# Graph network on one core: first score row spread by a product, constants taken behind the first exponentials, and identity products around seven stage boundaries

## The reference

```python
# network 0: x1 = relu(x @ W_ah + b_ah); three attention layers (4 heads of 192) on the same x1
h = (x1 @ W).reshape(N, H, C)
e = leaky_relu((h * a_src).sum(-1)[src] + (h * a_dst).sum(-1)[dst], 0.2)
p = exp(e - segment_max(e, dst)[dst])
out = segment_sum((p / (segment_sum(p, dst)[dst] + 1e-16))[:, :, None] * h[src], dst) + b
x = layernorm(x + relu(concat(relu(out_0), relu(out_1), relu(out_2)) @ W_out + b_out))
# network 1: one such layer with 4 heads of 512, elu, one with a single head of 768
x = layernorm(x + gat(elu(gat(x, heads=4, d=512)), heads=1, d=768))
```

## Time and profile before

| | us |
|---|---|
| median of 3 runs (1964.57 to 1966.22) | 1965.33 |
| the profiled execution | 1964.74 |
| its span | 1963.0 |
| TensorE busy in it | 1817.6 (93%) |
| VectorE busy | 1445.3 (74%) |
| ScalarE busy | 1034.1 (53%) |
| mean granted TensorE clock | 0.968 of 2.4 GHz |

### The profile page before, as it was taken

The page is one execution under the profiler, slowest core; times in us unless marked ns, Lnnn a source line. Parts: engine busy times, 40 slices in busy tenths (PEclk is TensorE's granted clock), DMA queues, the critical chain, the costliest instruction groups (busy, mean ns, idle before and its releaser), DMA issues. The chain is left out here.

```text
span 1963.0 us, 30340 instructions
## 1 busy us (share of the span) xinstructions
PE 1817.6 (93%) x11217; PEld 1754.5 (89%) x11217; DVE 1445.3 (74%) x2468; ACT 1034.1 (53%) x1631; POOL 135.3 (7%) x132
## 2 busy tenths in 40 slices
PE   7999899995999999997999899969999996999898
PEld 5777689995999999996999799969999996999798
DVE  7787659998989988984555559447888885346756
ACT  3666522215798898875211322257788874232633
POOL 5011022110000000000011011100000000000000
PEclk8999999997999999997999999989999998999899
DMA  4122154445284344537654566472342406545302
GB/s 123 52 62 67 35 154 138 116 118 133 62 210 100 100 110 101 132 72 197 182 172 147 143 188 192 141 190 66 118 140 68 133 27 183 166 122 129 101 9 79
DMA packets 181465, 234.72 MB, mean 120 GB/s; under 512 B 76102, under 2 KB 154288, under 8 KB 181083
## 3 DMA queue, kind: packets, MB, share of 16 engines
q1 hardware_dynamic: 173215, 205.31, 38.1%
q0 software_dynamic: 7216, 24.91, 4.4%
q10 hardware_dynamic: 902, 2.72, 0.5%
HBM read 167.89 MB, written 65.00 MB: 119 GB/s over the span
## 5 line engine op out<-in xcount | busy, mean ns | idle before, releaser
L1639 PE MATMUL p_o<-p_hi,h_parts 125*128 125x416 f32 (+1 forms) x960 | 282.7, 355 | 22.0 <-DVE p_lo L1573 15.5
L1089 PE MATMUL p_o<-first_room,p 125*125 125x193 f32 x1200 | 202.7, 330 | 13.2 <-DVE p L1045 10.4
L1089 PEld LDWEIGHTS p_o<-first_room,p 125*125 125x125 f32 x1200 | 197.9, 190 | 14.8 <-issue 14.3
L1639 PEld LDWEIGHTS p_o<-p_hi,h_parts 125*128 125x128 f32 x960 | 181.7, 189 | 28.2 <-issue 15.7
L1089 PE MATMUL p_o<-h_in,p 125*125 125x193 f32 x1200 | 198.1, 327 | 0.8 <-ACT res L976 0.8
L1089 PEld LDWEIGHTS p_o<-h_in,p 125*125 125x125 f32 x1200 | 196.0, 188 | 2.3 <-ACT res L976 1.2
L756 DVE CUSTOM_DVE_ANT_0 max_junk<-src_row,G 125x1250 bf16<-125x1250 f32 x120 | 186.2, 1623 | 9.9 <-DMA src_row<-score_rows 9.3
L1040 DVE TENSOR_TENSOR e<-e 125x1250 f32<-125x1250 f32 x120 | 174.3, 1452 | 20.0 <-ACT e L1002 19.9
L855 PE MATMUL p_h<-pw_hi,x1T 128*125 128x384 f32 x720 | 186.4, 340 | 0.0
L1045 DVE SCALAR_TENSOR_TENSOR p<-e,CT 125x1250 f32<-125x1250 f32 x120 | 175.3, 1461 | 4.1
L1375 PE MATMUL p_h<-pw_hi,x2T 128*125 128x256 f32 (+1 forms) x960 | 173.1, 282 | 0.0
(11 more groups left out here) (255 smaller groups left out, 3863.3 us busy)
## 6 DMA issues: line engine op xcount, KB each, us to landing
f_raw<-turned SPq DMA_DIRECT2D x40, 500.0 KB, 8.8
h_rows<-h_out SPq DMA_DIRECT2D x32, 560.0 KB
h_parts<-h_rows SPq DMA_DIRECT2D x40, 448.0 KB
turned<-tail_room SPq DMA_DIRECT2D x18, 625.0 KB, 7.3
G<-turned SPq DMA_DIRECT2D x20, 562.5 KB
h_rows<-h_out SPq DMA_DIRECT2D x24, 424.4 KB
first_room<-in_w_gat POOLq DMA_DIRECT2D x36, 192.0 KB, 2.7
first_room<-in_w_gat SPq DMA_DIRECT2D x6, 1152.0 KB
```

The lines of the kernel that those rows point to most:

```text
L1089: last = nc.tensor.matmul(p_o[:, b, n * 256:n * 256 + C0 + 1], p[:, g % RING, d * T:(d + 1) * T], h_in[hh][:, s, 0:C0 + 1], start=(s == 0 ...
L1639: last = nc.tensor.matmul(p_o[:, bank(n, c), 0:w], h[:, s, kind, cols].bitcast(F32R), pp[:, g % RING, 0:w], start=(s == 0 and j == 0), sto ...
```

## The change

Four kinds of edits.

- **First row.** In `project`, row 0 of the scores is spread by three f32 products of `rows` with column 0 of the identity as a broadcast stationary, and a copy by ScalarE into `src_row`, in place of its way over DRAM. Row 1 alone is still loaded by ScalarE's queue, now behind that copy. The split of `wa0` moves from the start of `project` on VectorE to the end of `counts_and_x1`.
- **Constants behind the first exponentials.** `aggregate_layer0` no longer waits for its bias before the first exponential; `aggregate_layer1` makes `ones` behind its first pair and `b_minus` behind its fourth. `project_layer1` has one extra exponential of a column at its 21st tile (`exp_of_one`), so that the activation table is there when `aggregate_layer1` begins. `aggregate_last` takes its first pair of exponentials before it rounds h, and the first `p_lo` before the next step of VectorE.
- **Identity products.** `keep_busy` writes ident x ident into a PSUM bank that nothing reads then: 8 at the end of stage 1; 12 at the start and 6 at the end of stage 3; 7 and 28 at those of stage 4; 9 and 40 at those of stage 6; 11 at the start of stage 7; 16 at the start of stage 8.
- **Constants of stage 1.** `ident_b` and `zeros_b` become slices of `band` (two memsets and a select less on GpSimd), and two small tiles lie in `G`'s room.

```diff
+def keep_busy(nc, ident, out, n):
+    for _ in range(n):
+        nc.tensor.matmul(out, ident[:, 0:out.shape[0]], ident[:], start=True, stop=True)
...
 # counts_and_x1, vector, at the end
+            dve.wait_ge(weighed.summed, weighed.chunks * 2 * weighed.heads)
+            v.tensor_copy(wa_hi[:], wa_flat).then_inc(wa_rounded, 1)
+            dve.wait_ge(wa_rounded, 1)
+            v.tensor_tensor(wa_lo[:], wa_flat, wa_hi[:].bitcast(F32), ALU.subtract)
...
 # project, scalar
             act.dma_start(score_rows[0:R, :], rows[:]).then_inc(rows_stored, 16)
+            act.wait_ge(row_spread, 1)
+            for b, (at, n) in enumerate(CH):
+                last = a.activation(src_row[:, 0, at:at + n], p_r[0:T, b, 0:n], ACT.Copy)
+            last.then_inc(row_in[0], 32)
             act.wait_ge(rows_stored, 16)
-            for h in range(2):
-                dma_in_two(act, src_row[:, h, :], score_rows[h:h + 1, :].broadcast_to([T, N]), row_in[h])
+            dma_in_two(act, src_row[:, 1, :], score_rows[1:2, :].broadcast_to([T, N]), row_in[1])
...
 # project, tensor
-            pe.wait_ge(wa_split, 1)
...
             last.then_inc(rows_turned, 1)
+            for b, (at, n) in enumerate(CH):
+                last = nc.tensor.matmul(p_r[0:T, b, 0:n], ident[0:R, 0:1].broadcast_to([R, T]), rows[:, at:at + n],
+                                        start=True, stop=True)
+            last.then_inc(row_spread, 1)
...
 # aggregate_layer0, scalar: the wait moves into keep(), in front of the first copy that needs the bias
-            act.wait_ge(bias_in, 16)
...
+                if i == 0 and c == 0:
+                    act.wait_ge(bias_in, 16)
...
 # project_layer1, scalar
+                if n == 2 * NT:
+                    a.activation(table_ahead[:], ident[0:T, 0:1], ACT.Exp)
...
 # aggregate_layer1, tensor, at the end (the other calls of keep_busy stand first or last in their lists)
+            pe.wait_ge(left, (ENDS - 1) * CW)
+            keep_busy(nc, core.ident, p_o[:, bank(ENDS - 2, CW - 1), 0:128], 40)
...
 # aggregate_last, vector
-                if g and s != 1:
+                if g == 0:
+                    rest_of_h(0)
+                    rest_of_p(0)
+                elif s != 1:
                     rest_of_p(g - 1)
                 add(g)
-                if s == 1:
+                if g == NT + 1:
                     rest_of_p(g - 1)
```

More of the change, by code:

```diff
@@ L217, in _ @@
                                pattern=[[1, NT]], channel_multiplier=-1).then_inc(later_ready, 1)
-            for m in (band, ident_b, zeros_b):
-                pool.memset(m[:], 0.0).then_inc(consts, 1)
-            pool.wait_ge(consts, 6)
-            pool.affine_select(out=ident_b[:], in_=ident_b[:], compare_op=ALU.not_equal, fill=1.0, base=0,
-                               pattern=[[-1, T]], channel_multiplier=1).then_inc(consts, 1)
+            pool.memset(band[:], 0.0).then_inc(consts, 1)
+            pool.wait_ge(consts, 4)
             pool.affine_select(out=band[:], in_=band[:], compare_op=ALU.not_equal, fill=1.0, base=N - T,
@@ L251, in _ @@
             step(v.scalar_tensor_tensor(meets[:, 0, :], least, tile_lo[:, 1:2], meets[:, 0, :], ALU.is_lt, ALU.mult))
-            step(v.scalar_tensor_tensor(meets[:, 1, :], run_no_i[:], float(-ER), meets[:, 0, :], ALU.add, ALU.mult))
-            step(v.scalar_tensor_tensor(meets[:, 2, :], run_no_i[:], 1.0, meets[:, 0, :], ALU.add, ALU.mult))
+            step(v.scalar_tensor_tensor(meets[:, 1, :], run_no_i, float(-ER), meets[:, 0, :], ALU.add, ALU.mult))
+            step(v.scalar_tensor_tensor(meets[:, 2, :], run_no_i, 1.0, meets[:, 0, :], ALU.add, ALU.mult))
             step(v.tensor_reduce(out=range_f[:, 2:3], in_=meets[:, 1, :], axis=AX.X, op=ALU.min))
@@ L787, in _ @@
             for b, (at, n) in enumerate(CH):
-                last = a.activation(rows[:, at:at + n], p_r[:, b, 0:n], ACT.Copy)
+                last = a.activation(rows[:, at:at + n], p_r[0:R, b, 0:n], ACT.Copy)
             last.then_inc(rows_kept, 1)
@@ L1491, in _ @@
             a = nc.scalar
-            act.wait_ge(ones_set, 1)
-            a.activation(ones[:], ones_f[:], ACT.Copy).then_inc(ones_set, 1)
-            act.wait_ge(bias_in, 16)
-            a.activation(b_minus[:], b_col[:], ACT.Copy, scale=-1.0).then_inc(bias_in, 16)
-            act.wait_ge(bias_in, 32)
             def round_p(g):
@@ L1533, in _ @@
                 last.then_inc(exp_ready, 1)
+                if g == 0:
+                    act.wait_ge(ones_set, 1)
+                    a.activation(ones[:], ones_f[:], ACT.Copy).then_inc(ones_set, 1)
                 if g:
                     round_p(g - 1)
+                if g == 3:
+                    act.wait_ge(bias_in, 16)
+                    a.activation(b_minus[:], b_col[:], ACT.Copy, scale=-1.0).then_inc(bias_in, 16)
+                    act.wait_ge(bias_in, 32)
                 if n and 4 <= s < 8:
@@ L1615, in sum_weights @@
             def sum_weights(g, n, s, w):
+                if g == 0:
+                    pe.wait_ge(ones_set, 2)
                 if s == 0:
@@ L2225, in _ @@
                 last.then_inc(exp_ready, 1)
-                if g:
+                if g == 0:
+                    round_h(0)
+                    round_h(1)
+                    round_p(0)
+                if g > 1:
                     round_p(g - 1)
@@ L2310, in _ @@
                 part, s = divmod(g, NT)
-                if part == 0:
+                if part == 0 and s:
                     rest_of_h(s)
@@ L2424, in gnn_two_layers @@
                 core.wa0 = sb1("wa0", [128, KD, 2, CONVS * H0], F32)
+                core.wa0_parts = [sb1(f"wa0_{name}", [128, KD, 2 * CONVS * H0], F32R) for name in ("hi", "lo")]
                 core.x1T = [sb1(f"x1T{i}", [128, KD, N], F32R) for i in range(2)]
                 counts_and_x1(nc, core, src, dst, x, w_ah, b_ah, w_gat0, a_gat0)
-                project(nc, core, core.x1T, w_gat0, core.wa0, h0_rows, score_rows, PAIR, cols[0:2], *cols[2:4])
+                project(nc, core, core.x1T, w_gat0, core.wa0_parts, h0_rows, score_rows, PAIR, cols[0:2], *cols[2:4])
             tail = ctx.enter_context(ExitStack())
```

53 lines of the change are left out of this document (31 added, 22 removed).

## The result

The changed kernel took 1957.13 us in the median of 7 runs (1954.44 to 1960.61), against 1966.88 for the kernel before in the same session (7 runs, 1964.57 to 1972.98): a ratio of 0.9948, 95% interval 0.9933 to 0.9962, 9.75 us or 0.5%. The profiled execution took 1956.66 us (span 1955.0), 8.1 less than that of before. The prediction had 17.85 us off that execution and 1947.5 us in all; the time came down as forecast, but by about half as much.

The account below looks back on a forecast made before the run. TensorE bounds the kernel, busy 1817.6 of 1963.0 us. Terms 5.1+1.8+2.3-0.2+3.15+1.7+4.0=17.85 off 1964.74 give 1946.9, plus 0.6 for the median 1947.5 us; range 1944 to 1951, 66 in 100.

Parts of the forecast that it names:

- Boundary 1 to 2 and stage 2, 5.1 us: Stage 2: first maximum 7.9 us earlier, TensorE's last tile 0.3 later, stage 3 begins 5.1 us earlier (2.5 to 6.5).
- Stage 3, 1.8 and 2.3 us: Start of stage 3: 1.8 us from not waiting for the bias, 2.3 us from the clock held by 12 identity products.
- The bias term: Start of stage 3: the first exponential no longer waits for `b_col`, 1.8 us gained.
- The clock term: Start of stage 3: 12 identity products spare TensorE's first products the 1.2 GHz clock, 2.3 us gained.
- Boundary 3 to 4 and stage 4, -0.2 and 0: Six products cost 0.2 us at the boundary; stage 4's faster start is worth nothing, as TensorE waits for `f_lo`.
- Stage 5, 0: Boundary 4 to 5: 28 products end beside SP's last stores; stage 5's first product hangs on VectorE: 0 (-0.3 to +0.3).
- Stage 6, 3.15 and 1.7 us: Start of stage 6: TensorE starts 3.15 us earlier with constants behind the exponentials; the held clock gives 1.7 us more.
- drain: Stage 6's table load: a skill's rule adds some 1380 ns, making the term 1.4 us larger; the prediction's trace disagreed.
- Stage 7, 0: Start of stage 7: 2.75 us at the low clock is worth nothing, as TensorE waits for `f_lo` behind a DMA.
- Stage 8, 4.0 us: Start of stage 8: 3.2 us earlier start, 1.75 us of clock, a 0.9 us wait; net 4.0 us (3.2 to 4.2).
- The identity products don't hold the clock: Rival, 14 in 100: in stages 2, 3, 6 and 8 only earlier starts count, 10.4 us, 1954.9 us.

Follow-up runs that it names:

- e8: The changed kernel without the six identity products ending stage 3 and the seven beginning stage 4: ratio 0.9959.
- e13: The kernel before with only the score-vector split moved to the end of stage 1 and the new stage 1 constants, first row over DRAM: 0.9986.
- e5: The kernel before with only the constants behind the first exponentials, the extra exponential in stage 5 and the new order of stage 8: 0.9957.
- e3: The changed kernel with all nine groups of identity products taken out: 0.9940.
- e10: The changed kernel with the first row over DRAM, first-head divisors ahead of the sums of weights, and no identity products: 0.9916.
- e18: The changed kernel run again unchanged, its third profile: 0.9957.
- e2: The changed kernel with VectorE making the first head's divisors ahead of two sums of weights: 0.9929.
- e4: The kernel before with only the nine groups of identity products put in: 0.9989.
- e7: The changed kernel with the first row sent over DRAM again: 0.9935, 1953.15 us.
- e15: The changed kernel with the first row over DRAM, first-head divisors first, and only the identity products 9, 40 and 11 of stages 6 and 7: 0.9942.

## Why the prediction was wrong, by its own steps

**Boundary 1 to 2 and stage 2, 5.1 us.** The steps held: first maximum at 260.82 (261.5 forecast), the new products at 2.35 us (3.8), VectorE's end 449.1 (450), SP's stores behind the last tile as what ends the stage. The term measured 3.5, 0.7 and 4.1 us in three profiles. What was too small was the delay of TensorE's tiles, 0.3 us forecast and 1.1, 4.1 and 0.9 measured from the stage's start; the range of the term, 2.5 to 6.5, missed one of three. In that one the new products ran at the low clock and took 4.50 us, in the others 2.35 and 2.34. The eight products behind stage 1 did not keep the clock either: it was at 0.50 for the first 3 us of stage 2 in two of the three (241.0 to 244.4 in the first).

**Stage 3, 1.8 and 2.3 us.** This is the step that failed: "VectorE needs 2.87 us for a step and TensorE 3.27, so the lead is not eaten." The rates are right and the conclusion is not, because the lead is eaten at the change of head, where TensorE waits for divisors and copies. From its first product to the second head it took 36.21 us (to 0.01) in all thirteen profiles that had VectorE's old order, whatever the clock was. I had read the waits there as for "VectorE or ScalarE work that follows its own products (bank copies)"; the 0.81 us of before followed VectorE's list. The bias term measured 1.42. The clock term measured not +2.3 but -2.7 to -3.1 against the first profile of before (-1.7 to -2.1 against the second), since the longer wait let the clock fall once more. In the profiled execution that is 5.0 of the 9.8 us that were missing (17.85 less 8.1).

**Boundary 3 to 4 and stage 4, -0.2 and 0.** -0.17 at the boundary. Stage 4 took 2.1 to 2.7 us more. The waits came for `fw_lo`, ahead of the `f_lo` that I had named; the length follows a transfer that lands at another time in different executions, and the products may add to it (e8). The reading of the earlier trace rows was off as well: 918.94 is where the last product before the wait starts, it lasts 0.34 us, and the wait up to 919.35 was under 0.1 us.

**Stage 5, 0.** +0.6 to +2.5 us in the changed kernel, +2.0 in e13, -0.04 in e5: scatter that the two profiles of before, both at the short end, did not show.

**Stage 6, 3.15 and 1.7 us.** 2.6 to the first product and 2.2, 2.2 and 0.7 behind it, 4.85 forecast and 4.8, 4.8 and 3.3 measured. e3, e5 and e10, without the nine products, have 0.2 to 0.3 in place of the 2.2: here the held clock is real, in two of three profiles. In the third the nine products left the clock at 0.50, and it rose 3.5 us behind the first real product (e18, timeline and windows):

```profile
1302.24 0.72 PE L1659 MATMUL p_o<-p_hi,h_parts 125*128 125x418 f32 x1 [0.78 <-DMA h_parts<-h_rows]
...
1302.00:1304.00 2.00, 1.76 (x5) 1.70 (x6) 1.94 (x4) 1.97 (x6) 0.00 (x0) 0.50 1.03 262
1304.00:1306.00 2.00, 2.00 (x7) 1.92 (x7) 1.97 (x5) 2.00 (x5) 0.00 (x0) 0.57 1.06 256
```

Of all eleven profiles with the nine products, six show 2.1 to 2.2 us there and five (e2, e4, e7, e15, e18) 0.3 to 0.7, each of those with 3.4 to 4.4 us at the low clock behind the first product or just after it. The table load is gone from the start, and no drain showed.

**Stage 7, 0.** -2.3, -0.4 and +0.2.

**Stage 8, 4.0 us.** 3.63 at the half, within the forecast range (start 3.13, wait 0.88 where 0.9 was forecast); then 1.8 to 2.0 are lost to a longer stretch at the low clock in two profiles of three. The 16 products' part in the 3.63 is 0.3 to 0.6; the order gives the rest (3.3 in e3, 3.1 in e10).

**The rivals.** "The identity products don't hold the clock" had nearly the right time (1954.9) for a wrong reason. They mostly hold it: 0.12 us a record where stage 1 ended, and no low clock at the first real products of stages 3, 4 and 8 in three profiles and of stage 6 in two. But what they hold is given back at the next wait: the 7 us that the real products of the changed kernel run faster (20.2 us lost to the low clock, 26.8 before) do not show in the time, as e3 is as fast.

## What to carry to other kernels

A lead is worth only what the next engine in line lets through: before pricing an earlier start or a faster clock, list every place where the engine waits for another one's list, also those with less than a microsecond, and ask whose position in time decides there. The same 36.21 us with a fast and a slow TensorE was the sign of it. Moving the divisors ahead of the sums of weights in VectorE's list mended the place in the timeline, though alone, on the kernel before, it gave nothing that could be told. And profile a kernel more than once: pieces that repeat to a hundredth can carry a sum, pieces that hang on transfers move by 2 to 3 us by themselves, as much as most terms here. Two profiles of the kernel before would have shown that for stages 1 and 2, but not for stages 4, 5 and 7, where only the other kernels did.

## What the hardware showed that I had not expected

The granted clock falls in a short wait too: in the 3.30 us of waiting from 498.4 to 501.7 it went to 0.50, until 507.2, and it fell in or just behind the same wait in all five profiles that had it, while waits of 0.81, 0.84, 1.54 and 1.78 us at the same place left it at 1.00. A change that lengthens one wait by 2.5 us can so cost 1.7 to 3.1 us more in what follows. And transfers scatter more than engines: the first row took 8.5 to 13.9 us over DRAM, the ninth chunk of weights came 12.4 to 15.4 us behind the start of its stage.
